# A Mamba, attention and expert block on one core: two layer norms' statistics move from VectorE to ScalarE and GpSimd, two router steps are fused, and the side stages get other places among the scan's units

## The reference

```python
xz = x @ in_proj_w.T ; u, res = split(xz)
u = silu(conv4(u)) ; dt, B, C = split(u @ x_proj_w.T)
delta = softplus(dt @ dt_proj_w.T + dt_proj_b)
h_t = exp(delta_t * A) * h_(t-1) + delta_t * B_t * u_t      # 512 channels x 16 states, 512 steps
y = (sum over states of h_t * C_t + u * D_skip) * silu(res) # then @ out_proj_w.T, + x, layer norm
q = gelu(l2norm(h @ q_w.T)) ; k = l2norm(h @ k_w.T) ; G = a weighted sum of q over the tokens
s = layernorm((G * k @ proj_w.T) * layernorm(h) @ fl_w.T + h)
f = layernorm(gelu(s @ d1_w.T) @ d2_w.T + s)
```

## Time and profile before

| | us |
|---|---|
| median of 3 runs (lowest, highest) | 7079.9 (7064.92, 7080.6) |
| the profiled execution | 7067.03 |
| its span | 7065.1 |
| recurrences (L1015), first and last start | 97.5 and 5971.9, 1024 of them |

### The profile page before, as it was taken

The page is one execution under the profiler, slowest core; times in us unless marked ns, Lnnn a source line. Parts: engine busy times, 40 slices in busy tenths (PEclk is TensorE's granted clock), DMA queues, the critical chain, the costliest instruction groups (busy, mean ns, idle before and its releaser), DMA issues. The chain is left out here.

```text
span 7065.1 us, 71122 instructions
## 1 busy us (share of the span) xinstructions
PE 5420.0 (77%) x16640; PEld 3017.2 (43%) x16640; DVE 5470.6 (77%) x7459; ACT 3698.5 (52%) x5660; POOL 4466.5 (63%) x2993
## 2 busy tenths in 40 slices
PE   4788888888888888878888888888888888599600
PEld 1344444444444444444444444444444444366400
DVE  5988888888888888888888888888888887211255
ACT  4555555555555555555555555555555653211155
POOL 3667677777667776767666767776767776300176
PEclk8898899998989888889999988999888888699855
DMA  7666666666666555655565655565556554022253
GB/s 261 229 195 204 197 203 205 206 200 209 199 204 206 200 189 199 200 192 197 197 200 186 203 191 198 197 203 199 197 192 201 198 189 168 24 86 86 88 155 93
DMA packets 492098, 1297.87 MB, mean 184 GB/s; under 512 B 59310, under 2 KB 216624, under 8 KB 490560
## 3 DMA queue, kind: packets, MB, share of 16 engines
q1 hardware_dynamic: 440960, 1219.82, 52.2%
q10 hardware_dynamic: 26048, 38.95, 1.6%
q0 software_dynamic: 24576, 33.72, 1.5%
HBM read 1206.19 MB, written 119.54 MB: 188 GB/s over the span
## 5 line engine op out<-in xcount | busy, mean ns | idle before, releaser
L485 POOL TENSOR_TENSOR st<-st,C_rows 128x1024 f32<-128x1024 f32 x1024 | 2462.3, 2410 | 732.2 <-DVE st L1015 729.4
L1015 DVE TENSOR_TENSOR_SCAN st<-dA,drive 128x1024 f32<-128x1024 f32 x1024 | 2337.0, 2282 | 127.5 <-ACT dA L665 45.8
L822 PE MATMUL y<-st,ident 128*128 128x512 f32 x4096 | 2120.5, 654 | 249.3 <-POOL st L485 239.6
L665 ACT ACTIVATE dA<-delta,a_neg 128x511 f32<-128x511 f32 x2048 | 1382.9, 713 | 1678.2 <-DVE st L1015 1671.1
L822 PEld LDWEIGHTS y<-st,ident 128*128 128x128 f32 x4096 | 834.0, 212 | 1280.4 <-issue 923.7
L987 DVE TENSOR_TENSOR drive<-du,B_rows 128x1024 f32<-128x1024 f32 x1024 | 1259.3, 1230 | 114.6 <-DVE du L982 26.2
L796 PE MATMUL pre_bank<-e_abs,in_w 128*128 128x512 f32 x1024 | 614.3, 732 | 235.7 <-DVE u L964 141.0
L1399 POOL DMA_INDIRECT rows<-expert_out,idx_c x256 | 268.8, 1050 | 620.3 <-DVE idx_c L1446 550.5
L776 PE MATMUL post_bank<-d_w,gT 128*128 128x256 f32 x2048 | 458.6, 380 | 26.4 <-issue 25.6
L567 POOL DMA_INDIRECT expert_in<-tb,idx x256 | 260.6, 1018 | 344.7 <-DVE idx_all L1174 283.6
L776 PEld LDWEIGHTS post_bank<-d_w,gT 128*128 128x128 f32 x2048 | 388.0, 190 | 123.4 <-issue 73.6
(11 more groups left out here) (197 smaller groups left out, 8066.0 us busy)
## 6 DMA issues: line engine op xcount, KB each, us to landing
B_rows<-bc_rows SPq DMA_DIRECT2D x1024, 512.0 KB
C_rows<-bc_rows SPq DMA_DIRECT2D x1024, 512.0 KB
xin<-in_x SPq DMA_DIRECT2D x32, 512.0 KB, 7.2
expert_in<-gT ACTq DMA_DIRECT2D x8, 2048.0 KB, 26.9
xn_rows<-xin SPq DMA_DIRECT2D x32, 512.0 KB, 6.2
h<-xn_rows SPq DMA_DIRECT2D x32, 512.0 KB, 6.5
x_res<-in_x SPq DMA_DIRECT2D x32, 512.0 KB, 3.6
x_rows<-x_res SPq DMA_DIRECT2D x32, 512.0 KB, 3.3
```

The source lines that it names most:

```text
L485: pool.tensor_tensor(tile[:, :, :], tile[:, :, :], bc[1][k % ROWS[1]][:, :, :], ALU.mult)\
L665: return act.activation(dA[k % 2][:, j, 1:L], delta[par][:, c, 1:L], ACT.Exp, scale=a_neg[:, c, n:n + 1])
L822: last = pe.matmul(Y[:, :], ident[:, :], st[k % RING][:, j, :], start=pair == 0 and j == 0, stop=pair == CU - 1 and j == 1)
L1015: dve.tensor_tensor_scan(st[k % RING][:, :, :].rearrange("p a l -> p (a l)"), dA[k % 2][:, :, :].rearrange("p a l -> p (a l)"), DR[:, :, : ...
```

## The change

Three things. **(1)** The statistics of x's norm and of the router's norm are no longer made on VectorE. ScalarE reads the four tiles with Identity and an accumulated output (the sums), GpSimd makes minus the mean of them, ScalarE reads the tiles again with Square and minus the mean as bias (the squares' sums), and GpSimd makes factor and shift, with as many instructions as before, in two portions. The written tiles are thrown away: into `rest` for x, into `tb` for the router. **(2)** Two comparisons of the router on VectorE (`pos2`, L1135, and `keep`, L1154) become the first operation of the instruction that used them. **(3)** Nearly all side stages get other places. Before and after, where they differ much or are spoken of:

| engine | stage: place before, place after |
|---|---|
| SyncE | load of x 10, 2; its store 24, 26; store of B and C rows 50, 56; load of h 7, 6; load of x for the router 56, 59; store of x1 29, 41; wait for the scattered tokens 55, 47 |
| TensorE | x turned 24, 27; in_proj 27 29 32 34 37 39 42 44, 28 28 29 35 40 42 47 47; x_proj 47, 48; dt_proj 50 51 52 53, 51 51 54 55; h turned 23, 26; q 26, 28; k 30, 31; G 45, 49; fl 65, 62; d1 79 81 86 88, 79 84 89 93; d2 1 3 13 15, 0 0 12 13; n turned 35, 40; dots 37, 41; running sums 42, 43 |
| VectorE | x stats 19, gone; router's stats 30, gone; conv 30 32 35 37, 29 34 37 37; delta 72 76, 85 91; gate 3 6, 3; first sum of f 7, 15; f normed 21, 19; stats of o 23, 20; q sum 29, 28; second stats of h 31, 35; qw 41, 43; t 59, 56; s 69, 67; router 39 41 44, 42 42 43 |
| ScalarE | x: sums 6, squares 13 (new), normed 22, 22, turned 26, 22; conv's first tap 29 31 34 36, 25 28 32 33; silu of u, g0, g1 41, 43; g2, g3 46, 44; xd 49, 50; z 52 53 54 55, 51 58 58 58; softplus 57 to 66, 58 to 68; h normed 21, 15; s normed 73, 70; gelu 84 91, 86 95; first decay of the next sequence 95, 93; router: sums 27, squares 31 (new), normed 33, 36, turned 36, 38, Exp 40, 41 |
| GpSimd | x 20, 10 and 22; h's factor 19, 17; softplus 61 63 68 70, 67 68 72 84; x1 28, 26; router's factor 31, 31 in two portions; s_g and s_b 1 and 4, 5 and 5; eight indirect transfers 44 45 46 47 50 51 52 53, all at 43 |

```diff
@@ attention_phase
-        stat_pre = sb("stat_pre", [P, TT, 6])
-        mv_pre = sb("mv_pre", [P, TT, 2])
+        sum_pre = sb("sum_pre", [P, TT])
+        sq_pre = sb("sq_pre", [P, TT])
+        sum_late = sb("sum_late", [P, TT])
+        sq_late = sb("sq_late", [P, TT])
@@ gpsimd
+            def mean_of(steps, name, shifted, total):
+                pool.sem_inc(carried_pool, 1)
+                pool.tensor_scalar(shifted[:, :], total[:, :], -1.0 / D, None, ALU.mult).then_inc(steps.did(f"{name}_m"), 1)
+            def scale_of(steps, name, out, shifted, squares, eps, b):
+                pool.sem_inc(carried_pool, 1)
+                pool.tensor_scalar(out[:, :], squares[:, :], 1.0 / D, eps, ALU.mult, ALU.add)\
+                    .then_inc(steps.did(f"{name}_v"), 1)
...
             def pre(b, par):
-                yield 20
-                pool.wait_ge(*pre_dve.at("x_aggr", b))
-                scale_and_shift(pre_pool, "x", r_pre, shift_pre, mv_pre, LN_EPS, b)
+                at = iter((10, 22, 67, 68, 72, 84))
+                yield next(at)
+                pool.wait_ge(*pre_act.at("x_sum", b))
+                mean_of(pre_pool, "x", shift_pre, sum_pre)
+                yield next(at)
+                pool.wait_ge(*pre_act.at("x_sq", b))
+                scale_of(pre_pool, "x", r_pre, shift_pre, sq_pre, LN_EPS, b)
...
@@ scalar
+            def sum_of(junk, src, total):
+                for tile in range(TT):
+                    last = act.activation(junk(tile), src[:, tile, :], ACT.Identity, accum_out=total[:, tile:tile + 1])
+                return last
+            def squares_of(junk, src, minus_mean, total):
+                for tile in range(TT):
+                    last = act.activation(junk(tile), src[:, tile, :], ACT.Square, bias=minus_mean[:, tile:tile + 1],
+                                          accum_out=total[:, tile:tile + 1])
+                return last
             def pre(b, par):
-                yield 22
+                at = iter((6, 13, 22, 22, 25, 28, 32, 33, 43, 44, 50, 51, 58, 58, 58, 58, 58, 64, 64, 67, 68, 93))
+                yield next(at)
+                act.wait_ge(x_loaded, 16 * (b + 1))
+                act.wait_ge(*pre_pool.at("log1p2", b - 1))
+                sum_of(junk, xin, sum_pre).then_inc(pre_act.did("x_sum"), 1)
+                yield next(at)
+                act.wait_ge(*pre_pool.at("x_m", b))
+                act.wait_ge(*pre_act.at("x_sum", b))
+                squares_of(junk, xin, shift_pre, sq_pre).then_inc(pre_act.did("x_sq"), 1)
...
             def late(b):
+                at = iter((25, 27, 31, 36, 38, 41))
...
+                act.wait_ge(*late_pool.at("x1", b))
+                sum_of(lambda tile: tb[:, tile, :], x_res, sum_late).then_inc(late_act.did("n_sum"), 1)
+                yield next(at)
+                act.wait_ge(*late_pool.at("n_m", b))
+                act.wait_ge(*late_act.at("n_sum", b))
+                squares_of(lambda tile: tb[:, tile, :], x_res, shift_late, sq_late).then_inc(late_act.did("n_sq"), 1)
...
@@ vector
-                yield 19
-                dve.wait_ge(x_loaded, 16 * (b + 1))
-                stats(pre_dve, "x", tiles_of(xin), stat_pre, mv_pre, b)
...
-                yield 30
-                dve.wait_ge(*late_pool.at("x1", b))
-                stats(late_dve, "n", tiles_of(x_res), stat_late, mv_late, b)
...
-                dve.tensor_scalar(pos2[:, :], wts[:, :, 1], 0.0, None, ALU.is_gt).then_inc(late_dve.did("pos2"), 1)
...
-                dve.tensor_tensor(oh[1][:, :, :], oh[1][:, :, :], pos2[:, :].unsqueeze(2).to_broadcast([P, TT, NE]),
-                                  ALU.mult).then_inc(late_dve.did("oh1_pos"), 1)
+                dve.scalar_tensor_tensor(oh[1][:, :, :], wts[:, :, 1:2].to_broadcast([P, TT, NE]), 0.0, oh[1][:, :, :],
+                                         ALU.is_gt, ALU.mult).then_inc(late_dve.did("oh1_pos"), 1)
...
-                dve.tensor_scalar(keep[:, :, :], cum[:, :, :], float(CAP), None, ALU.is_le)\
-                    .then_inc(late_dve.did("keep"), 1)
...
-                dve.tensor_tensor(cum[:, :, :], cum[:, :, :], slot0[:, :].unsqueeze(1).to_broadcast([P, TT, NE]),
+                dve.tensor_tensor(slotv[:, :, :], cum[:, :, :], slot0[:, :].unsqueeze(1).to_broadcast([P, TT, NE]),
                                   ALU.add).then_inc(late_dve.did("slotv"), 1)
                 dve.wait_ge(*late_dve.at("slotv", b))
-                dve.tensor_tensor(cum[:, :, :], cum[:, :, :], keep[:, :, :], ALU.mult)\
+                dve.scalar_tensor_tensor(cum[:, :, :], cum[:, :, :], float(CAP), slotv[:, :, :], ALU.is_le, ALU.mult)\
                     .then_inc(late_dve.did("slotk"), 1)
```

More of the change, by code:

```diff
@@ L231, in attention_phase @@
         wts = sb("wts", [P, TT, 2])
-        pos2 = sb("pos2", [P, TT])
         oh = [sb(f"oh{i}", [P, TT, NE]) for i in range(2)]
@@ L235, in attention_phase @@
         cum = sb("cum", [P, TT, NE])
-        keep = sb("keep", [P, TT, NE])
         pick = [sb(f"pick{i}", [P, TT, NE]) for i in range(2)]
+        slotv = sb("slotv", [P, TT, NE])
         slot_f = sb("slot_f", [P, TT, 2])
@@ L259, in attention_phase @@
         zeroed = sem("zeroed")
-        pre_dve = Steps(sem("pre_dve"), ["x_stats", "x_aggr"]
-                        + [f"conv{c}_{j}" for c in range(KI) for j in range(3)]
+        pre_dve = Steps(sem("pre_dve"), [f"conv{c}_{j}" for c in range(KI) for j in range(3)]
                         + ["delta0", "delta2"])
-        pre_act = Steps(sem("pre_act"), ["x_normed", "xT"] + [f"tap{c}" for c in range(KI)] + ["u"]
+        pre_act = Steps(sem("pre_act"), ["x_sum", "x_sq", "x_normed", "xT"] + [f"tap{c}" for c in range(KI)] + ["u"]
                         + [f"g{c}" for c in range(KI)] + ["xd"] + [f"z{c}" for c in range(KI)] + ["z_abs", "sp_exp0", "sp_exp2", "sp_w0", "sp_w2", "sp_m0", "sp_m2", "sp_ln0", "sp_ln2"])
@@ L286, in attention_phase @@
                             "f_g", "f_normed", "o_stats", "o_aggr",
-                                            "n_stats", "n_aggr", "dots", "top", "top_i", "dv", "top_f", "w1", "w2", "pos2", "oh0", "oh1",
-                            "oh1_pos", "asg", "w_all", "cum", "keep", "run", "slotv", "slotk", "pick0", "pick1",
+                                            "dots", "top", "top_i", "dv", "top_f", "w1", "w2", "oh0", "oh1",
+                            "oh1_pos", "asg", "w_all", "cum", "run", "slotv", "slotk", "pick0", "pick1",
                             "slot0", "slot1", "idx", "idx_all"])
@@ L408, in late @@
             def late(b):
-                yield 29
+                at = iter((41, 47))
+                yield next(at)
                 sp.wait_ge(*late_pool.at("x1", b))
@@ L461, in scale_and_shift @@
                     .then_inc(steps.did(f"{name}_shift"), 1)
-            def pre(b, par):
-                yield 20
-                pool.wait_ge(*pre_dve.at("x_aggr", b))
-                scale_and_shift(pre_pool, "x", r_pre, shift_pre, mv_pre, LN_EPS, b)
-                for c, slot in ((0, 61), (2, 63)):
-                    yield slot
+            def mean_of(steps, name, shifted, total):
[5 more added lines that the diff above has]
+                    .then_inc(steps.did(f"{name}_v"), 1)
+                pool.wait_ge(*steps.at(f"{name}_v", b))
+                pool.tensor_tensor(out[:, :], out[:, :], minus_half[:, 0:out.shape[1]], ALU.pow)\
+                    .then_inc(steps.did(f"{name}_r"), 1)
+                pool.wait_ge(*steps.at(f"{name}_r", b))
+                pool.tensor_tensor(shifted[:, :], shifted[:, :], out[:, :], ALU.mult)\
+                    .then_inc(steps.did(f"{name}_shift"), 1)
+            def pre(b, par):
+                at = iter((10, 22, 67, 68, 72, 84))
+                yield next(at)
+                pool.wait_ge(*pre_act.at("x_sum", b))
+                mean_of(pre_pool, "x", shift_pre, sum_pre)
+                yield next(at)
+                pool.wait_ge(*pre_act.at("x_sq", b))
+                scale_of(pre_pool, "x", r_pre, shift_pre, sq_pre, LN_EPS, b)
+                for c in (0, 2):
+                    yield next(at)
                     pool.wait_ge(*pre_act.at(f"sp_m{c}", b))
@@ L471, in pre @@
                         .then_inc(pre_pool.did(f"rest{c}"), 1)
-                for c, slot in ((0, 68), (2, 70)):
-                    yield slot
+                for c in (0, 2):
+                    yield next(at)
                     two = e_abs[:, c:c + 2, :]
@@ L628, in pre @@
                         .then_inc(pre_act.did(f"z{c}"), 1)
-                yield 57
+                yield next(at)
                 act.wait_ge(*pre_act.at("z3", b))
                 act.activation(e_abs[:, :, :], delta[par][:, :, :], ACT.Abs).then_inc(pre_act.did("z_abs"), 1)
-                for c, slot in ((0, 58), (2, 60)):
-                    yield slot
+                for c in (0, 2):
+                    yield next(at)
                     act.wait_ge(*pre_act.at("z_abs", b))
```

(13 more changed lines are left out.)

185 lines of the change are left out of this document (100 added, 85 removed).

## The result

The changed kernel takes **6733.6 us** (median of 4 runs, 6730.9 to 6745.1) against 7077.4 of the kernel before: 0.952 of it, interval 0.9504 to 0.9537. The forecast was 6850, range 6660 to 7045: sign and range hold, but -230 was forecast and -344 came.

What follows compares the result with a forecast made beforehand. VectorE's work, about 161 us a sequence, sets the pace, plus some twenty us where its neighbours are late. Terms sum to -7.8 us a sequence, -234 over 30, +4 for the last two: 6850 us forecast, range 6660 to 7045.

Steps and rivals of the forecast that it cites:

- Statistics off VectorE, -3.7 a sequence: VectorE's queue: statistics of x (1.83 us) and the router (1.85 us) leave uncovered places, so they go in full.
- ScalarE's 7.2 us at nothing: ScalarE: new sums and squares take 7.2 us a sequence, covered by its idle stretches of 2.9 us before the decays.
- Gates, -4.4: VectorE's gates: first gate's wait for TensorE gone, third's shortened, -4.4 of 9.4 us a sequence.
- New waits at the recurrences, +3.5: Recurrences wait for ScalarE's decay(12), queued behind more work, and its earlier request for g2: +3.5 us a sequence.
- The step on delta: Sequence's end: delta at 85 and 91 gives TensorE's adds time, shrinking idle before recurrences: -1.0 us, from -3 to +1.
- The eight transfers: GpSimd, all at 43 before times_c(14) and (15): gate 1 left as it is, 0, with ends -3 and +3.3.
- The sum of f, unchanged: VectorE's sum of f: stays as late as it was (99.1 us of idle), since d2 ends at 13 instead of 15.
- The work that leaves VectorE: VectorE: both statistics and the fused steps, -3.9 us a sequence; busy time falls by about 120 us.
- only the work counts: Rival: new places win and lose equally, leaving -3.9 x 30 = -117, 6963 us; chance 0.2.
- Nothing changes: Rival: TensorE is the bound and each us taken from VectorE returns at a gate, 7080 us; chance 0.06.
- ScalarE holds the decays: Rival: ScalarE asks early for TensorE's late results, holding three decays a sequence, +144, 7224 us; chance 0.1.
- the transfers' rule: GpSimd's transfers: rule against their new place; 1.31 us apart usually, one waited 4.07 us unreleased; range reaches over it.

Runs made afterwards that it cites:

- experiment 1: Kernel before with only the statistics of x's and the router's norm moved to ScalarE and GpSimd, old places, router steps not fused: 6977.0 us, 0.9864.
- experiment 3: Changed kernel with both statistics back on VectorE, x's at place 9 and the router's at 30, new places and fused steps kept: 6818.4 us, 0.9651.
- experiment 9: Changed kernel with both statistics on VectorE (x's at 9), the eight transfers spread over 44 to 53 and SyncE's wait at 55: 6669.9 us, 0.9482.
- experiment 11: Changed kernel with ScalarE's sums of x and of the router made twice, 2 x 1.6 us more work a sequence: 6745.7 us, 0.9546.
- experiment 5: Changed kernel with delta's two VectorE steps at 73 and 78 instead of 85 and 91, GpSimd's last delta step at 75 instead of 84: 6768.1 us, 0.9578.
- experiment 10: Changed kernel with only SyncE's wait for the scattered tokens back at 55 instead of 47, the eight transfers left at 43: 6725.7 us, 0.9519.
- experiment 2: Changed kernel with both statistics back on VectorE, at 19 and 30, new places and fused steps kept: 6922.2 us, 0.9782.
- experiment 4: Kernel before with one GpSimd step, the addition of the row lni_b, moved from place 42 to 56, away from dv: 7125.3 us, 1.007.

## Why the prediction was right in sign and short in size

- **Statistics off VectorE, -3.7 a sequence: right.** 113.1 us of work went, 3.5 a sequence, and experiments 1, 3 and 9 value it at 96, 93 and 126 us (87 by the times alone in the last). **Fused steps, -0.2:** too small to be seen.
- **ScalarE's 7.2 us at nothing: right** as far as experiment 11 tells, which added 3.2 and lost some 18 us. The new instructions take 226 us of it, as forecast (230), but its busy time rose by 142.9: table loads fell from 443 to 381, 79.5 us, 31 of them before the decays (186 before, 155 now, 39.7 us), by the order alone.
- **Gates, -4.4: right but for a little.** 300.0 to 181.7 is -3.7. As forecast, gate 0's wait went (88.3 to 3.4 us) and gate 2's shrank (45.8 to 8.8). **Conv, -3.0:** 103.8 to 26.3 is -2.4.
- **New waits at the recurrences, +3.5, less 1.0 at the end of the sequence: right in sum, by luck.** 127.5 to 201.5 is +2.3. But the idle for ScalarE's decays, which should have made the +3.5, rose by 21.3 us only (45.8 to 67.1, 0.7 a sequence). 25.3 more are idle with nothing that the trace shows as their end ("issue"), and that for TensorE ("PE y"), which should have shrunk, rose by 9.2; the cause of the rest is open. The step on delta had the wrong mechanism too. Its new places gain because they don't meet GpSimd: 24.3 us less of work than before, 66.2 less than at 73 and 78 (experiment 5).
- **Router, +1.0: right.** `dots` +25.4 and the reciprocal of the weights +11.5 make 36.9, 1.15 a sequence, inside the 0.5 to 2 stated.
- **SyncE's wait, nothing: right** (experiment 10).
- **The eight transfers, "I leave gate 1 as it is, 0": right against the kernel before and mis-costed all the same.** Gate 1 kept its wait (161.3 us before, 164.9 after, over 32 sequences). But TensorE was no longer late there by itself: spread, the wait falls to 26.9. The bounds were -3 and +3.3, taken around a gate that stays; the bunching hid a gain of some 150 us, 5 a sequence, including 34.8 us of a wait of `ssg` that was not in the sum.
- **The sum of f, unchanged: wrong.** 99.1 to 48.0, 51 us. All of it is the second of its two halves, at place 18 (61.8 to 10.3). Experiment 2 has it too (14.2) and experiment 1 has not (66.1), so it comes from the places; which of them is open. That the waiting came out near -117 in total is partly luck: this gain was not in the sum, and neither was `ssg`'s new wait of 38.9 us.
- **The step that failed: the work term.** "The work that leaves VectorE" counted what was removed and took the length of everything that stays from one trace as given. It was -120 and is -231; 134.1 of it are collisions that no longer happen. For `dv` experiment 4 shows it and for `delta` experiment 5; for `du` and `wts` the grouping by GpSimd's instructions does, and experiment 2 shows that the places alone bring it about. (By groups the statistics' 113.1, the two comparisons' 11.2 and the 134.1 come to 258 us; the busy time fell by 230.6, mainly because neighbouring instructions overlap and the groups' times do not quite add up to it.) The row was there to be read: VectorE's `dv`, 128x4, at 1572 ns.

The rivals: "only the work counts" (6963) falls, since experiment 3 gives the places more than the work. "Nothing changes" and "ScalarE holds the decays" fall with the result; for ScalarE the recurrences wait 67.1 us, where even the forecast had over 100. What the range calls the transfers' rule, a wait of 4.07 us as in the earlier trace rows in each of 30 sequences, would be 122 us. It did not come. Of 224 transfers behind another (the first of each eight left out) two started over 1 us late with nothing that released them before (4.07 and 1.24 us), and two after (3.22 and 5.31). After, `du`, with both inputs in SBUF, ran beside 58 of these transfers or the gaps ahead of them, and but for the one of 5.31 us these gaps were 0.30. TensorE's clock over the sequence is 0.91 (0.90 before), as expected above 0.90. A sequence takes 172.5 us (5519 us from first to last recurrence through 32 sequences), not 179; since the mean before was 183.6 and not the 187 of the one stretch of the earlier trace rows, that is -11.1 where -7.8 was forecast.

## What to carry to other kernels

Before the durations of a trace go into a sum, compare each with its shape: where the same form is sometimes twice as long, it collides, and a change of order changes it, without touching it. When a chain is rearranged, ask of a term that is "as late as before" what it would be without the new obstacle; a bunch of small instructions in front of the one that a reader waits for can eat a good part of the gain (here some 150 of 494 us). Here the changed order with the old spread of the transfers beats both kernels, 6582.9 us against 6733.6 and 7077.4.

## What was not expected of the hardware

- A VectorE subtraction of 128x4 took 1.61 us for 0.15 under a GpSimd instruction, with both inputs in SBUF, and a 128x512 product up to 5.26 for 0.67, through two GpSimd instructions one behind the other. With one input in PSUM nothing lengthened (`drive`, 1.23 us at most, 827 times under GpSimd).
- The wait is passed on: the GpSimd addition behind such a VectorE instruction took 3.34 us for 2.34 (experiment 5). In the kernel before, GpSimd's multiplication of h (`h<-h,row_ln_g`) beside a `du` took 2.8 to 2.9 us for 2.35, and `du` kept its 0.67, 30 times.
- Of 224 indirect transfers behind another in each kernel, two at most started 3 to 5 us late with nothing that released them (3.22 and 5.31 us after, 4.07 before). The cause is open.
